# The same megakernel with its SBUF tiles declared in another order

## The reference

```
x = x + tanh(g_xattn[0]) * L0_xattn(ctx, ctx, layernorm(x))   # A: 16 heads, softmax over the heads
x = x + tanh(g_ffn[0])   * L0_ffn(layernorm(x))               # B: down(silu(gate(x)) * up(x)), hidden 768
x = x + tanh(g_xattn[1]) * L1_xattn(layernorm(x), ctx)        # C: 16 query heads, one key/value head
x = x + tanh(g_ffn[1])   * L1_ffn(layernorm(x))               # D: x W.T + b and a low-rank term
```

## Time and profile before

| what | us |
|---|---|
| median of 3 runs | 2447.99 |
| profiled execution, span of its instructions | 2442.8 |
| lead-in, the 58 rounds, drain, in that span | 163, 2106, 173 |
| PE busy | 2357.7 (97%) |
| DVE, POOL, ACT busy | 2205.6, 1773.4, 1719.5 |

### The profile page before, as it was taken

How to read it: one execution, slowest core, us unless ns; L and a number is a source line. 1 busy time by engine, 2 the same in 40 slices (tenths; PEclk the granted TensorE clock), 3 DMA queues, 4 the chain that set the end, 5 groups by cost and what they waited for, 6 DMA issues and landing times.

```text
span 2442.8 us, 70142 instructions
## 1 busy us (share of the span) xinstructions
PE 2357.7 (97%) x27814; PEld 2081.6 (85%) x27814; DVE 2205.6 (90%) x3678; ACT 1719.5 (70%) x3402; POOL 1773.4 (73%) x2512
## 2 busy tenths in 40 slices
PE   6899999999999999999999999999999999999897
PEld 5788888888888888888888888888888888888786
DVE  6879999999999999999999999999999999999963
ACT  4567777777777777777777777777777777777664
POOL 3667777777777777787777777777777777777653
PEclk9999999999999999999999999999999999999999
DMA  3000010010011010011001000001001001101000
GB/s 106 25 19 29 28 35 24 28 35 24 28 35 30 22 35 30 26 31 30 28 28 30 28 28 31 28 28 35 24 28 35 24 28 35 30 22 35 17 19 15
DMA packets 74326, 73.26 MB, mean 30 GB/s; under 512 B 6555, under 2 KB 73393, under 8 KB 74290
## 3 DMA queue, kind: packets, MB, share of 16 engines
q1 hardware_dynamic: 74290, 72.75, 9.5%
HBM read 54.90 MB, written 16.78 MB: 29 GB/s over the span
## 4 chain that ended last, share of the span: by engine, by line
PE 64%; DVE 19%; ACT 7%; POOL 7%; issue 2%; DMA 0%; POOLq 0%; SPq 0%; DVEq 0%; ACTq 0%
PE work L2136 13%; PE work L2137 11%; PE work L2138 11%; DVE m L1517 6%; PE scores L2229 6%; PE scores L2239 5%; PE work L2272 5%; PE work L2175 4%; DVE scores L1523 4%; ACT e L857 3%; POOL zt L417 3%; PE scores L2218 3%; ACT xn_D L814 3%; PE work L2153 2%; PE work L2159 2%
## 5 line engine op out<-in xcount | busy, mean ns | idle before, releaser
L857 ACT ACTIVATE e<-scores 120x1024 f32<-120x1024 f32 x512 | 513.4, 1029 | 88.3 <-PE scores L2239 56.6
L2136 PE MATMUL work<-xt_hi_B,w_hi 128*128 128x256 f32 x1536 | 456.5, 297 | 3.8 <-DVE y_lo_A L1497 1.6
L2137 PE MATMUL work<-xt_lo_B,w_hi 128*128 128x256 f32 x1536 | 430.2, 280 | 0.0
L2138 PE MATMUL work<-xt_hi_B,w_lo 128*128 128x256 f32 x1536 | 430.0, 280 | 0.0
L417 POOL TENSOR_TENSOR zt<-e 120x512 f32<-120x512 f32 x256 | 328.7, 1285 | 118.1 <-ACT e L857 112.1
L411 POOL TENSOR_TENSOR h_lo<-h_f,h_hi 128x256 fp32r<-128x256 f32 x384 | 279.5, 735 | 147.3 <-ACT h_hi L807 147.1
L1517 DVE TENSOR_REDUCE m<-scores 120x128 fp32r<-120x2048 f32 x128 | 291.0, 2273 | 66.2 <-PE scores L2229 66.0
L2136 PEld LDWEIGHTS work<-xt_hi_B,w_hi 128*128 128x128 f32 x1536 | 289.3, 188 | 60.6 <-DVE h_f L1511 24.9
L1523 DVE TENSOR_TENSOR scores<-scores,m 120x1024 f32<-120x1024 f32 x256 | 302.8, 1227 | 4.3
L1535 DVE TENSOR_TENSOR e<-e,work 120x2048 f32<-120x2048 f32 x128 | 291.4, 2277 | 0.2
L2137 PEld LDWEIGHTS work<-xt_lo_B,w_hi 128*128 128x128 f32 x1536 | 289.9, 189 | 0.0
(11 more groups left out here) (256 smaller groups left out, 7283.5 us busy)
## 6 DMA issues: line engine op xcount, KB each, us to landing
x_ln<-xp SPq DMA_DIRECT2D x64, 256.0 KB, 2.7
x_res<-xp SPq DMA_DIRECT2D x64, 256.0 KB, 2.7
y<-y_out SPq DMA_DIRECT2D x64, 256.0 KB, 2.2
ctx_f_A<-cp SPq DMA_DIRECT2D x64, 128.0 KB, 2.5
ctx_f_C<-cp SPq DMA_DIRECT2D x64, 128.0 KB, 2.0
qm<-mT SPq DMA_DIRECT2D x256, 4.0 KB
e<-wi SPq DMA_DIRECT2D x3, 768.0 KB, 5.5
w_ctx<-wc SPq DMA_DIRECT2D x1, 656.0 KB
```

The costliest lines, as they stand in the source:

```text
L857: return act.activation(e[0:SC, c, 2 * h:2 * h + 2, :, :].rearrange("p a b n -> p (a b n)"), scores[0:SC, 2 * h:2 * h + 2, :].rearrange("p ...
L2136: pe.matmul(out, a_hi, b_hi_, start=first, stop=False, skip_group_check=parts)
L2137: pe.matmul(out, a_hi, b_lo_, start=False, stop=False, skip_group_check=parts)
L2138: last = pe.matmul(out, a_lo, b_hi_, start=False, stop=end, skip_group_check=parts)
```

## The change

The declarations of the 97 SBUF tiles are put in another order. No tile is added, dropped or resized, and no instruction of any engine is changed or moved: the five engines' programs are the same row for row, with line numbers shifted by one. What changes is the address of nearly every tile. `w_hi` and `w_lo` stay where they were. `parity` and `row_of` (together 64 bytes with their rounding) come next, so that all large tiles then begin 64 bytes further than the weights, by multiples of 256; the small tiles that had shifted this go to the end. `v1_one` (128 bytes) is put ahead of `xt_hi` and `xt_lo` of A, B and C, which shifts these six and `w_ctx` by another 128.

Start of the tiles, modulo 256 bytes (worked out from the order and the sizes; slices of the weights, `xt`, `y` and `h` tiles begin multiples of 512 bytes further):

| tiles | before | after |
|---|---|---|
| `w_hi`, `w_lo` | 128 | 128 |
| `xt_hi`, `xt_lo` of A, B, C | 32 | 64 |
| `xt_hi_D`, `xt_lo_D` | 32 | 192 |
| `y_hi`, `y_lo`, `h_hi`, `h_lo`, `y1f`, `th`, `act_g`, `h_f` | 192 | 192 |
| `qt_A`, `kz0`, `kz1`, `km1`, `qm1`, `ctx_f`, `v0_pad`, `v1_one` | 192 | 192 |
| `e0`, `e1`, `zt`, `m0`, `m1`, `mT` | 64 | 192 |
| `x_ln`, `x_res`, `x1` to `x3`, `y_out`, `xn_*`, `xt_*` | 32 | 192 |
| `ident`; `wk0`; `w_ctx` | 128; 160; 0 | 192; 192; 64 |

From it the distance by which the stationary tile begins behind the moving one, modulo 256:

| product | before | after |
|---|---|---|
| `gate_up`, `queries` A and C | 96 | 64 |
| `rows_out` D | 160 | 64 |
| `down`, `rows_out` A and C | 64 | 64 |
| `keep_busy` | 0 | 0 |
| scores (all) | 0 | 0 |
| attended values (start of the tiles) | 128 | 0 |
| transposes of `xn_*`; of `m1` | 160; 192 | 0; 0 |

Modulo 512 the distance of `gate_up` and the `queries` is 96 before and 320 after; that of `down` and the other `rows_out` is 64 before and after, and that of `rows_out` D becomes 64.

```diff
@@ -90,24 +90,17 @@
 
         w_hi = sb("w_hi", [P, WCOLS], F32R)
         w_lo = sb("w_lo", [P, WCOLS], F32R)
+
+        parity = sb("parity", [P, 2])
+        row_of = sb("row_of", [P, 4])
+
         ident = sb("ident", [P, P])
-        masks = sb("masks", [P, 2])
         neg_ident = sb("neg_ident", [P, P], F32R)
         wk0 = sb("wk0", [P, KC * D])
-        parity = sb("parity", [P, 2])
-        row_of = sb("row_of", [P, 4])
-        neg_row = sb("neg_row", [P, 2])
-        w_ctx = sb("w_ctx", [P, CCOLS])
         ones_k = sb("ones_k", [P, D], F32R)
-        bias_col = sb("bias_col", [P, 2 * KC])
-        key_bias = sb("key_bias", [P, 2, KC])
         bias_rows = sb("bias_rows", [P, 2, D])
         x3_biased = sb("x3_biased", [P, NT, D])
         val_bias = sb("val_bias", [P, D])
-        minus_half = sb("minus_half", [P, NT])
-        eps_tile = sb("eps_tile", [P, NT])
-        zero_tile = sb("zero_tile", [P, NT])
-
         x_ln = sb("x_ln", [P, NT, D])
         x_res = sb("x_res", [P, NT, D])
         x1 = sb("x1", [P, NT, D])
@@ -115,11 +108,46 @@
         x2_before = sb("x2_before", [P, NT, D])
         x3 = sb("x3", [P, NT, D])
         y_out = sb("y_out", [P, NT, D])
-
         xn = {s: sb(f"xn_{s}", [P, NT, D]) for s in "ABCD"}
         xt = {s: sb(f"xt_{s}", [P, KC, S]) for s in "BCD"}
-        xt_hi = {s: sb(f"xt_hi_{s}", [P, KC, S], F32R) for s in "ABCD"}
-        xt_lo = {s: sb(f"xt_lo_{s}", [P, KC, S], F32R) for s in "ABCD"}
+        ctx_f = {s: sb(f"ctx_f_{s}", [P, KC, P]) for s in "AC"}
+        qt = {st: sb(f"qt_{st}", [P, KC * S]) for st in "A"}
+        kz0 = sb("kz0", [P, 2, KC, P])
+        kz1 = sb("kz1", [P, 2, P])
+        km1 = sb("km1", [P, 2, P])
+        qm1 = sb("qm1", [P, 2, KC * S])
+        v0_pad = sb("v0_pad", [P, H // 2, 64])
+        m0 = sb("m0", [P, 2, P], F32R)
+        m1 = sb("m1", [P, 2, P])
+        mT = sb("mT", [P, S])
+        e0 = sb("e0", [P, NT, 4, 4, P])
+        e1 = sb("e1", [P, KC, 4, 2, S])
+        zt = sb("zt", [P, NT, 8, P])
+        z0 = sb("z0", [P, NT, P])
+        yz_q = sb("yz_q", [P, KC, 2, S // 32, 2 * HD])
+        y_q = sb("y_q", [P, KC, S // 32, 2, HD])
+        y1f = sb("y1f", [P, KC, S])
+        y_hi = {s: sb(f"y_hi_{s}", [P, KC, S], F32R) for s in "AC"}
+        y_lo = {s: sb(f"y_lo_{s}", [P, KC, S], F32R) for s in "AC"}
+        th = sb("th", [P, 2, S])
+        act_g = sb("act_g", [P, 2, S])
+        h_f = sb("h_f", [P, 2, S])
+        h_hi = sb("h_hi", [P, HC, S], F32R)
+        h_lo = sb("h_lo", [P, HC, S], F32R)
+        xt_hi = {"D": sb("xt_hi_D", [P, KC, S], F32R)}
+        xt_lo = {"D": sb("xt_lo_D", [P, KC, S], F32R)}
+
+        v1_one = sb("v1_one", [P, 2 * HD])
+        xt_hi.update({s: sb(f"xt_hi_{s}", [P, KC, S], F32R) for s in "ABC"})
+        xt_lo.update({s: sb(f"xt_lo_{s}", [P, KC, S], F32R) for s in "ABC"})
+        w_ctx = sb("w_ctx", [P, CCOLS])
+
+        neg_row = sb("neg_row", [P, 2])
+        bias_col = sb("bias_col", [P, 2 * KC])
+        key_bias = sb("key_bias", [P, 2, KC])
+        minus_half = sb("minus_half", [P, NT])
+        eps_tile = sb("eps_tile", [P, NT])
+        zero_tile = sb("zero_tile", [P, NT])
         stats = {s: sb(f"stats_{s}", [P, NT, 6]) for s in "ABCD"}
         mv = {s: sb(f"mv_{s}", [P, NT, 2]) for s in "ABCD"}
         var_eps = {s: sb(f"var_eps_{s}", [P, NT]) for s in "ABCD"}
@@ -127,38 +155,11 @@
         neg_mean = {s: sb(f"neg_mean_{s}", [P, NT]) for s in "ABCD"}
         shift = {s: sb(f"shift_{s}", [P, NT]) for s in "ABCD"}
         rstd = {s: sb(f"rstd_{s}", [P, NT]) for s in "ABCD"}
-
-        ctx_f = {s: sb(f"ctx_f_{s}", [P, KC, P]) for s in "AC"}
-
-        qt = {st: sb(f"qt_{st}", [P, KC * S]) for st in "A"}
-        kz0 = sb("kz0", [P, 2, KC, P])
-        kz1 = sb("kz1", [P, 2, P])
-        km1 = sb("km1", [P, 2, P])
-        qm1 = sb("qm1", [P, 2, KC * S])
-
-        v0_pad = sb("v0_pad", [P, H // 2, 64])
-        v1_one = sb("v1_one", [P, 2 * HD])
-        m0 = sb("m0", [P, 2, P], F32R)
-        m1 = sb("m1", [P, 2, P])
-        mT = sb("mT", [P, S])
-
-        e0 = sb("e0", [P, NT, 4, 4, P])
-
-        e1 = sb("e1", [P, KC, 4, 2, S])
-        zt = sb("zt", [P, NT, 8, P])
-        z0 = sb("z0", [P, NT, P])
-        yz_q = sb("yz_q", [P, KC, 2, S // 32, 2 * HD])
         rz_q = sb("rz_q", [P, KC, 2, S // 32])
-        y_q = sb("y_q", [P, KC, S // 32, 2, HD])
-        y1f = sb("y1f", [P, KC, S])
+        tg = sb("tg", [P, 4])
+        graw = sb("graw", [P, 4])
+
         bias_row = y1f[0:1, :, :].rearrange("p k n -> p (k n)")
-        y_hi = {s: sb(f"y_hi_{s}", [P, KC, S], F32R) for s in "AC"}
-        y_lo = {s: sb(f"y_lo_{s}", [P, KC, S], F32R) for s in "AC"}
-        th = sb("th", [P, 2, S])
-        act_g = sb("act_g", [P, 2, S])
-        h_f = sb("h_f", [P, 2, S])
-        h_hi = sb("h_hi", [P, HC, S], F32R)
-        h_lo = sb("h_lo", [P, HC, S], F32R)
 
         e0_flat = e0[:, :, :, :, :].rearrange("p a b c d -> p (a b c d)")
         e1_flat = e1[:, :, :, :, :].rearrange("p a b c d -> p (a b c d)")
@@ -172,8 +173,6 @@
         t2_s = e1_flat[0:50, small + 3 * D:small + 4 * D]
         ldT_s = e1_flat[0:100, small + 4 * D:small + 4 * D + 4]
         luT_s = e1_flat[0:4, small + 4 * D + 4:small + 4 * D + 54]
-        tg = sb("tg", [P, 4])
-        graw = sb("graw", [P, 4])
 
 
         scores = ctx.enter_context(nc.psum_tensor("scores", [P, 4, 512], F32))
```

More of the change, by code:

```diff
@@ L120, in flamingo_kernel @@
         xt = {s: sb(f"xt_{s}", [P, KC, S]) for s in "BCD"}
-        xt_hi = {s: sb(f"xt_hi_{s}", [P, KC, S], F32R) for s in "ABCD"}
-        xt_lo = {s: sb(f"xt_lo_{s}", [P, KC, S], F32R) for s in "ABCD"}
-        stats = {s: sb(f"stats_{s}", [P, NT, 6]) for s in "ABCD"}
-        mv = {s: sb(f"mv_{s}", [P, NT, 2]) for s in "ABCD"}
-        var_eps = {s: sb(f"var_eps_{s}", [P, NT]) for s in "ABCD"}
-        ln_count = sb("ln_count", [P, 1])
-        neg_mean = {s: sb(f"neg_mean_{s}", [P, NT]) for s in "ABCD"}
-        shift = {s: sb(f"shift_{s}", [P, NT]) for s in "ABCD"}
-        rstd = {s: sb(f"rstd_{s}", [P, NT]) for s in "ABCD"}
         ctx_f = {s: sb(f"ctx_f_{s}", [P, KC, P]) for s in "AC"}
@@ L150, in flamingo_kernel @@
         yz_q = sb("yz_q", [P, KC, 2, S // 32, 2 * HD])
-        rz_q = sb("rz_q", [P, KC, 2, S // 32])
         y_q = sb("y_q", [P, KC, S // 32, 2, HD])
         y1f = sb("y1f", [P, KC, S])
-        bias_row = y1f[0:1, :, :].rearrange("p k n -> p (k n)")
         y_hi = {s: sb(f"y_hi_{s}", [P, KC, S], F32R) for s in "AC"}
@@ L161, in flamingo_kernel @@
         h_lo = sb("h_lo", [P, HC, S], F32R)
+        xt_hi = {"D": sb("xt_hi_D", [P, KC, S], F32R)}
[10 more added lines that the diff above has]
+        zero_tile = sb("zero_tile", [P, NT])
+        stats = {s: sb(f"stats_{s}", [P, NT, 6]) for s in "ABCD"}
+        mv = {s: sb(f"mv_{s}", [P, NT, 2]) for s in "ABCD"}
+        var_eps = {s: sb(f"var_eps_{s}", [P, NT]) for s in "ABCD"}
+        ln_count = sb("ln_count", [P, 1])
+        neg_mean = {s: sb(f"neg_mean_{s}", [P, NT]) for s in "ABCD"}
+        shift = {s: sb(f"shift_{s}", [P, NT]) for s in "ABCD"}
+        rstd = {s: sb(f"rstd_{s}", [P, NT]) for s in "ABCD"}
+        rz_q = sb("rz_q", [P, KC, 2, S // 32])
+        tg = sb("tg", [P, 4])
+        graw = sb("graw", [P, 4])
+        bias_row = y1f[0:1, :, :].rearrange("p k n -> p (k n)")
         e0_flat = e0[:, :, :, :, :].rearrange("p a b c d -> p (a b c d)")
```

## The result

| kernel | median, us | lowest to highest | ratio to before, 95% interval | profiled span |
|---|---|---|---|---|
| before | 2448.23 | 2446.66 to 2448.75 (5 runs) | | 2442.8 |
| after | 2435.5 | 2433.65 to 2436.58 (5 runs) | 0.9948 [0.9938, 0.9959] | 2433.5 |

The change makes the kernel 12.7 us faster by the medians (10 to 15 us by the interval), and 9.3 us by the two profiled executions. The two figures differ because the profiled execution of before was a quick one: an execution takes 2.0 us more than its span in the profile of after, so that one took about 2445, 3 us under its median.

What follows compares the result with a forecast made beforehand. PE (64% of the chain) was taken to bound the kernel between the `xn_D` wait and the last attended values; 0.38 - 0.05 - 0.08 = 0.25 us a round over 60 rounds, 15 us, gave span 2428, so 2433 us, range 2425 to 2451.

Steps and rivals of the forecast that it cites:

- `queries` A: Query products of layer A, distance 96 to 64: 11 steps at 113.5 ns, 1.25 us against 1.30, gaining 0.05 us a round.
- `rows_out` D: Output product of layer D, distance 160 to 64: 12 steps, 1.36 us against 1.43, gaining 0.07 us a round.
- `gate_up`, 68 steps: The 72 gate_up products without first ones: 68 steps from 117.3 to 113.5 ns, gaining 0.26 us a round.
- entries of five streams: Starts of fp32r streams on the path: each loses three steps at 3.8 ns before the fast pace, 0.05 us a round.
- wait for the exponential takes over: End of gate_up's first stretch: of 0.13 us saved there a third counts, 0.08 us a round lost to PE's wait for ACT.
- The mechanism: PE's fp32r streams: weight load and moving stream hold each other up in SBUF; distance 64 allows 113.5 ns a step.
- the products off the path: PE's `queries` C, `down` and `rows_out` C: any change of pace falls in slack ahead of the `xn_D` wait, worth nothing.
- Plain float32 products: Scores, attended values and transposes on PE: nothing taken; bounds 7 us lost for attended values, 4 us for transposes.
- rival 1: gate_up streams, which start behind scores, mostly stay at 117.5 ns; a third of the gain, 5 us: 2443 us; chance 0.20.
- DVE, ACT and POOL: Their tiles move to multiples of 64 bytes: durations unchanged to 1%, at most 5 us either way.
- 2: Addresses don't matter; paces of PE's streams come from what stands around them: 2448 us, no gain; chance 0.13.
- 3: Distance counts modulo 512 or more, so gate_up and `queries` A get 320, a worse one: slower, 2459 us; chance 0.12.

Runs made afterwards that it cites:

- PE-only kernel: Kernel with the computation left out: PE alone runs streams of 24 fp32r products at varied operand distances; 113.3 to 120.0 ns a step in steps of 32 bytes.
- B alone: The changed kernel with the xt tiles of A and C at 192 modulo 256 and those of B still at 64; 2435.68 us, ratio to before 0.995.
- A and C alone: The changed kernel with the xt tiles of B back at distance 96 and those of A and C at 64; 2447.35 us, ratio to before 0.9995.

## Why the prediction was right, and where not

It said 2433 and the median is 2435.5; the gain was forecast at 15 us and is 12.7 by the medians and 9.3 by the traces. That the total comes so near is in part luck: the round was to lose 0.25 us and lost 0.155, and the profiled span was forecast at 2428 us and is 2433.5. The 5.2 us by which before's profiled span lay under its median were added to the forecast; in after that difference is 2.0. Step by step, in us a round:

| step | predicted | measured |
|---|---|---|
| `queries` A | -0.05 | +0.006 |
| `rows_out` D | -0.07 | -0.020 |
| `gate_up`, 68 steps | -0.26 | -0.21 |
| entries of five streams | +0.05 | 0.15, contained in the three rows above |
| wait for the exponential takes over | +0.08 | +0.06 |
| `rows_out` A, transposes, `down`, `queries` C, key scores | 0 | +0.01 in all |
| sum | -0.25 | -0.155 |

- *The mechanism* was right: the distance sets the pace of the fp32r streams, shown by the PE-only kernel and by B alone against A and C alone.
- *`gate_up`* was right in pace, in the size of the gain and in the share that the wait for the exponential takes. Of 34 steps x 3.8 ns = 0.13 us in its first half, 0.04 came through: 0.06 went into two waits (the step between its two pieces from 117 to 138 ns, the step into the scores from 265 to 302), 0.03 into slow steps. The next 24 gave 0.084 of 0.09, the last 12 gave 0.026 of 0.04.
- *The mis-sized term is the entries.* The step read: "five streams with three steps at 3.8 ns are 0.05 us". Some streams do lose just a few steps (in the PE-only kernel behind plain products, say), but one that misses the fast pace doesn't fall into it after three steps; it stays at 117.8 for its whole length. That was to be seen in the earlier trace rows, which I put down as rival 1 for `gate_up` and not for the two short products. In the prediction's sum this is 0.106 us a round (0.056 and 0.050), 6 us. What `rows_out` D, at distance 64 each time, finds is set by the stream ahead of it: 117.8 behind A at 64, 113.3 behind A at 192.
- Even so, the 0.05 for D would have added little on top of a fast `gate_up`: with D fast as well, the time stayed. That is how the sum failed a second time. I let savings ahead of the scores of A count in full and added them to those of `gate_up`; of 42 ns won there 4 to 18 were left beside a fast `gate_up`, and 38 beside a slow one. The exponential was said to move with them, and beside a fast `gate_up` it did so only in part; DVE's slack in the round, 0.42 us before and 0.07 after, points to DVE, and no run settles it.
- *At nothing* I had put the products off the path. Their paces did change (`down` +65 ns, `queries` C -44), and the wait for `xn_D` took it up (-28), which leaves -7. *Plain float32 products* have the same durations at the new distances, so the bounds of 7 and 4 us are empty, and the 385 against 400 ns of the earlier trace rows are not the distance, which is now 0 for both. The width of the stationary tile, which the prediction named, is left as the likely reason; no run varies it alone. *DVE, ACT and POOL* unchanged to 1%.
- The rivals: 1 (entries decide for `gate_up`) was not so, though it was so for the streams before it; 2 and 3 fell with the PE-only kernel and the measured time. The Trainium skill ("TensorE: Matmul & The Clock Gate", Part 2, step by step) says that loading the next weights takes no read bandwidth from the running matmul. Read as the prediction read it, it would give these streams one pace, and the trace of the PE-only kernel doesn't agree: with no other engine at work, the pace goes from 113.3 to 120 ns with the addresses of the two operands. That it is read bandwidth which one takes from the other isn't shown; no run leaves the weight loads out.
- The signs named ahead: `gate_up` at 113.5, yes; `rows_out` D at 113 to 114, no; round 36.0 to 36.1, it is 36.15; the step into the scores behind the first 36, from 265 to 302 ns where 206 is unwaited, so the wait grew from 0.06 to 0.10 and not to 0.15.

What stays open: what in the hardware makes the pace hang on distance and phase; and 3 us between the difference of the medians and that of the traces, which lie within what single executions of one kernel differ by (up to 8 us here). A hint on these: before and A, C alone at 64 have the same round (36.309 and 36.308 us), yet profiled spans of 2442.8 and 2445.5 us, which points to the stretches ahead of and behind the loop, where before's execution would have been quick.

## What to carry to other kernels

When streams of one shape run at different paces in a trace, list the start addresses of both operands beside the paces: here the difference modulo 256 bytes explained most of it, and moving two tiles was worth 0.5%. Before counting a fast pace for every stream, look whether some stream with the same addresses is slow for its whole length: then the pace is a state that a stream can miss. A saving on PE ahead of a wait for the softmax can be worth a fraction: a quarter to a third of it in `gate_up`'s first half, and in `rows_out` D from a tenth to nearly all, depending on whether `gate_up` was fast already. Savings of this kind need not add up, so each is to be tried with and without the other. Of what stands behind that wait, the next 24 products came through nearly whole.

## What the runs showed of the hardware

- fp32r products of 128 x 128 by 256 columns have a pace that depends on the distance of their operands' starts modulo 256 bytes, from 113.3 to 120 ns in steps of 32 bytes, and up to 130 in steps of 8. At distance 64 the absolute place makes no difference (both tiles 32 to 224 bytes on: 113.3 throughout); at other distances this wasn't tried.
- Distance 64 has two stable paces, 113.3 and 117.8 ns. Which one a stream takes is settled in its first few products: with 1, 4, 5 or 8 plain products ahead it is fast, with 2, 3, 6 or 7 slow, and it stays so over 24 products. The products just ahead don't decide alone: behind the same batch of scores the same stream was slow (117.8) and fast (113.3), with another stream ahead of the scores. Distance 144 was the only other one to reach 113.3, in one case after ten slow steps.
- The stream ahead decides what the next one finds, and not by its own pace being fast: `down`, at 64 all along, went from 113.4 to 117.8 when the stream ahead of it (`queries` C) became faster, and back when that was slowed again.
